# An expert's weights fetched in four pieces of 32 partitions, one piece per finished tile

## The reference

```
xn = layernorm(x)
x  = x + attention(xn) + ffn(xn)            # attention: 16 heads of 32, one shared K and V, causal
scores = sigmoid(xn @ gate_w.T)             # 32 experts in 4 groups; 2 groups, then 8 experts per token
x_lat  = xn @ fc1_w.T                       # 512 -> 256
h      = relu(x_lat @ w1[e].T) ** 2         # 256 -> 256, for each chosen expert e
y_lat += weight[token, e] * (h @ w2[e].T)   # 256 -> 256, summed over the 8 experts of a token
ffn    = y_lat @ fc2_w.T + relu(xn @ up.T) ** 2 @ down.T
```

## Time and profile before

| | |
|---|---|
| median of three runs | 1802.2 us |
| the profiled execution's own time | 1801.09 us |
| its span | 1799.3 us |
| TensorE (PE) busy | 1642.5 us, 91% |
| VectorE (DVE) busy | 1196.9 us, 67% |
| ScalarE (ACT) busy | 1068.8 us, 59% |
| GpSimd (POOL) busy | 825.5 us, 46% |
| moved by the 16 DMA engines | 277.86 MB, mean 154 GB/s |
| mean granted TensorE clock | 0.974 |

### The profile page before, as it was taken

One profiled execution on the slowest core, in us unless ns is written; L12 is line 12 of the kernel. 1 busy time (PEld: TensorE's weight loads), 2 busy tenths in 40 slices (PEclk: granted clock), 3 DMA queues, 4 the chain that ended last, 5 costly groups with the idle time before them and its releaser, 6 DMA issues.

```text
span 1799.3 us, 40017 instructions
## 1 busy us (share of the span) xinstructions
PE 1642.5 (91%) x10806; PEld 1389.0 (77%) x10806; DVE 1196.9 (67%) x3661; ACT 1068.8 (59%) x2791; POOL 825.5 (46%) x670
## 2 busy tenths in 40 slices
PE   5833999999999999999999998999999999999989
PEld 5822777777777777787777776888888988889977
DVE  6868877767868778677677784454445544455557
ACT  2322775766757757677577574666556665566642
POOL 0042532433424424334244241577677766777850
PEclk9966999999999999999999999999999999999999
DMA  7983533434334334334343334688888887888894
GB/s 279 369 308 79 153 99 117 143 103 130 124 98 144 116 110 137 106 123 132 97 149 119 122 99 138 145 162 178 171 182 171 168 181 167 175 169 153 138 258 164
DMA packets 189150, 277.86 MB, mean 154 GB/s; under 512 B 34232, under 2 KB 130623, under 8 KB 186372
## 3 DMA queue, kind: packets, MB, share of 16 engines
q0 software_dynamic: 60352, 92.59, 23.9%
q1 hardware_dynamic: 73636, 117.19, 22.0%
q10 hardware_dynamic: 54944, 65.52, 12.4%
HBM read 123.93 MB, written 131.76 MB: 142 GB/s over the span
## 4 chain that ended last, share of the span: by engine, by line
PE 57%; DMA 14%; DVE 12%; issue 7%; ACT 2%; POOL 1%; DVEq 1%; POOLq 0%; ACTq 0%; SPq 0%
DMA sums<-e_y,e_where 13%; PE m_psT L1190 7%; PE e_psH L1566 6%; PE e_psY L1577 6%; PE m_psU L64 5%; PE m_psU L66 4%; PE m_psU L65 4%; PE m_psS L1173 4%; PE m_psO L1210 4%; PE m_psY L64 4%; PE m_psY L66 4%; PE m_psY L65 4%; DVE m_sc L999 3%; PE e_psX L1551 2%; POOL sums L1531 1%
## 5 line engine op out<-in xcount | busy, mean ns | idle before, releaser
L1531 POOL DMA_INDIRECT sums<-e_y,e_where x287 | 445.7, 1553 | 202.7 <-DVE e_y L1490 123.7
L777 POOL DMA_INDIRECT slot_rows<-m_row,slots x256 | 268.4, 1048 | 553.0 <-ACT m_sc L854 509.0
L854 ACT ACTIVATE m_sc<-m_sc,m_low 128x512 f32<-128x512 f32 (+3 forms) x512 | 283.8, 557 | 154.8 <-DVE m_low L999 153.5
L1577 PE MATMUL e_psY<-e_w,e_ht 128*128 x1148 | 302.8, 387 | 25.9 <-ACT e_ht L1438 25.9
L1566 PE MATMUL e_psH<-e_xt,e_w_of 128*128 128x128 f32 x2296 | 310.3, 279 | 3.3 <-ACT e_xt L1427 3.3
L999 DVE CUSTOM_DVE_ANT_0 m_sc<-m_psS,cst 128x512 f32<-128x512 f32 (+3 forms) x512 | 229.6, 485 | 90.8 <-PE m_psS L1173 89.6
L1566 PEld LDWEIGHTS e_psH<-e_xt,e_w_of 128*128 128x128 f32 x2296 | 283.4, 194 | 5.6 <-ACT e_xt L1427 4.0
L1433 ACT ACTIVATE e_w_of<-e_w 128x512 f32 x287 | 180.8, 630 | 130.9 <-issue 122.4
L1577 PEld LDWEIGHTS e_psY<-e_w,e_ht 128*128 128x128 f32 x1148 | 198.8, 193 | 45.8 <-issue 29.6
L1487 DVE TENSOR_SCALAR e_where<-e_row,e_shifts 128x1 uint32<-128x1 uint32 x287 | 61.4, 214 | 214.0 <-DMA sums<-e_y,e_where 180.4
L1190 PE MATMUL m_psT<-cst,m_sc 128*128 128x128 f32 x1280 | 199.8, 277 | 2.0 <-ACT m_pt L865 2.0
(11 more groups left out here) (201 smaller groups left out, 3162.8 us busy)
## 6 DMA issues: line engine op xcount, KB each, us to landing
e_row<-slot_rows ACTq DMA_DIRECT2D x287, 144.5 KB, 3.5
m_qs<-m_qhi SPq DMA_DIRECT2D x256, 64.0 KB, 2.0
e_w<-in_w SPq DMA_DIRECT2D x64, 256.0 KB, 4.6
f_xt<-in_x SPq DMA_DIRECT2D x8, 1024.0 KB, 9.3
xnt_hi<-f_hi SPq DMA_DIRECT2D x8, 1024.0 KB, 4.4
xnt_lo<-f_lo SPq DMA_DIRECT2D x8, 1024.0 KB, 7.7
m_qs<-m_qlo SPq DMA_DIRECT2D x128, 64.0 KB, 2.0
sums<-empty POOLq DMA_DIRECT2D x32, 256.0 KB
```

The costliest lines, as they stand in the source:

```text
L777: pool.indirect_dma_start(out=xs, out_offset=bass.IndirectOffsetOnAxis(ap=slots_sb[:, g, k:k + 1], axis=0), in_=row[g % 2][:, :], in_offse ...
L854: nc.scalar.activation(cols, cols, ACT.Exp, bias=low[:, h % 2, i:i + 1], scale=-1.0, accum_out=total[:, h % 2, i:i + 1]).then_inc(exp_done, 1)
L1531: pool.indirect_dma_start(out=both_sums, out_offset=bass.IndirectOffsetOnAxis(ap=where[u % NY][:, 0:1], axis=0), in_=y[u % NY][:, :], in_o ...
L1577: mm = pe.matmul(psY[u % 2][:, 0:LAT], ht[u % 2][:, c * P:(c + 1) * P], w_f[:, bass.ds(e * (2 * W) + (W + c * LAT), LAT)], start=(c == 0), ...
```

## The change

An expert's two weight DMAs of 128 partitions become eight of 32 partitions. The four pairs are issued one after another; for experts 5 to 31 the pair q (q = 0, 1, 2, 3) waits until q further tiles have finished after the last tile of expert k-5. The first five experts' pieces are issued without waits between them. The two loads of `partial` follow the fourth pair, and so move back by three tiles. The semaphore count that `arrived` waits for is four times as high. Nothing else is changed.

```diff
+WP = 4
...
+            def load_part(k, q):
+                cols, rows_of = slice(k * W, (k + 1) * W), slice(q * P // WP, (q + 1) * P // WP)
+                for n, w in enumerate((w1, w2)):
+                    sp.dma_start(w_sb[rows_of, k, n, :], w[rows_of, cols]).then_inc(w_in[k % 2], 16)
+
             def load(k):
-                cols = slice(k * W, (k + 1) * W)
-                for n, w in enumerate((w1, w2)):
-                    sp.dma_start(w_sb[:, k, n, :], w[:, cols]).then_inc(w_in[k % 2], 16)
+                for q in range(WP):
+                    load_part(k, q)
 
             def arrived(k):
-                sp.wait_ge(w_in[k % 2], 32 * (k // 2 + 1))
+                sp.wait_ge(w_in[k % 2], 32 * WP * (k // 2 + 1))
                 sp.sem_inc(w_ready, 1)
...
             for k in range(AHEAD, E):
                 arrived(k - 1)
-                sp.wait_ge(y_done, end_of(k - AHEAD) + BASE)
-                load(k)
+                end = end_of(k - AHEAD)
+                for q in range(WP):
+                    sp.wait_ge(y_done, end + (BASE + q))
+                    load_part(k, q)
```

## The result

The changed kernel takes **1781.71 us** (median of five runs, 1779.58 to 1787.75) against 1802.2. The ratio to the kernel before is 0.989 with a 95% interval of 0.9857 to 0.9923: 20 us faster, and clear of no change. Measured once more on another chip it was 1780.73 us, ratio 0.988 (0.9851 to 0.991). Its profiled execution has a span of 1779.8 us.

What follows compares the result with a forecast made beforehand. Overrun, then idle DMA engines delayed scatters, costing the experts' stage 40 us against TensorE's pace. Work of 393 + 23 + 16 = 432 us at share 0.965 gives 448 instead of 468: 1801 - 20 = 1781 us, range 1760 to 1808.

Steps and rivals of the forecast that it cites:

- Work: Experts' stage: DMA engine time after the change, 393 us plus 23 for narrow width and 16 for starts, 432 us.
- the price of a piece: Weight loads: a narrow 128 KB piece (two DMAs) costs 0.56 us instead of 0.34, plus 0.10 us a DMA for starts.
- The row for the width: Attention's 64 KB query moves, nearest in shape to a narrow DMA: 236 GB/s at full share against 384 for 128 partitions.
- Share: Experts' stage: the DMA engines can hold 0.965, the middle of 0.92 without a stall and 1.01 in a burst.
- the burst of 768 KB: Weights and partial issued together: a scatter lands in 7.74 us instead of 3.41, holding VectorE, GpSimd and then TensorE.
- SyncE: Issuing queue: each issue takes about 0.42 us, six more an expert 2.5 us, hidden by 322.9 us of waits for tiles.
- The 512 KB without a stall: Last weight load, at 1618.74: the chain stays on TensorE, which speaks for bursts below 512 KB costing nothing.
- VectorE's wait for scatters: Sign in the experts' stage: the wait of VectorE's address step should fall well below 153.0 us.
- Landing of a piece: Sign at the weight loads: 2 to 3 us expected; over 5 us would speak for the pieces clogging the engines.
- No difference: Rival: starts cost 0.19 us a DMA, gain 5 us, 1796 us; or partial loads cause the stalls; chance 0.31.
- All hidden: Rival in the experts' stage: the whole 40 us loss is gained, 1761 us; chance 0.18.
- Slower: Rival at each expert's first four tiles: pieces and starts clog the DMA engines, 27 us more, 1828 us; chance 0.16.

Runs made afterwards that it cites:

- f1: Against the kernel before: eight weight DMAs of 128 partitions (64 KB each) an expert, all issued without waits for tiles; 1776.93 us, ratio 0.9852.
- e1: Against the kernel before: eight weight DMAs of 32 partitions an expert, all issued without waits for tiles; 1783.77 us, ratio 0.989.
- e2: Against the kernel before: w1 whole at the end of expert k-5, w2 whole two tiles later, then partial; 1791.25 us, ratio 0.993.
- f2: Against the kernel before: two whole weight DMAs at once, only the loads of partial moved back, by four tiles (the second by five); 1793.84 us, ratio 0.994.
- h2: Against the kernel before: four weight DMAs of 64 partitions (128 KB) an expert, without waits for tiles; 1795.46 us, ratio 0.9957.
- m1: Against the kernel before: sixteen weight DMAs of 16 partitions (32 KB) an expert, without waits for tiles; 1787.04 us, ratio 0.991.
- e4: Against the changed kernel: partial one tile after the fourth piece, the second load another tile later; 1777.86 us, ratio 0.9854 to the kernel before.
- i1: Against the changed kernel: each load of partial in four DMAs of 32 partitions at its old place; 1776.66 us, ratio 0.9851 to the kernel before.
- g1: Against the changed kernel: four 128 KB weight DMAs of 128 partitions, one per tile, and partial one tile later; 1775.77 us, ratio 0.9855 to the kernel before.

## Why the prediction was right, and where only its number was

**The time.** 1781 was forecast, 1781.71 measured, inside the forecast's own range of 1768 to 1790. Two terms of the sum were wrong, and cancelled.

- *Work.* 432 us of DMA time were expected for 217 tiles. It was 0.91 x 452 = 411 for 218: the change added some 18 us to the 393 (the rounding of the shares leaves about 5 either way), not 39. The term that was mis-sized is the price of a piece, 0.56 for its width and 0.20 for two starts. The row for the width was of moves within SBUF in a stretch that has little else; beside scatters and row loads it does not hold: eight wide DMAs and eight narrow ones used the same 1.85 us of DMA time a tile (f1, e1), and their times differ by no more than the noise. Their 0.03 us a tile over the kernel before is 6 us or so for 162 more DMAs, 0.04 each, where I took 0.10; the changed kernel's 18 is 0.11 each, and why it is more there than in e1 is open. The Trainium skill ("SBUF — State Buffer", section "Door 1: The DMA port swizzle") gives measured rates for 32 and 128 partitions, 189 and 328 GB/s; beside this kernel's other traffic that difference does not show.
- *Share.* I divided by 0.965, between a stretch without stall and a burst. Over the stage the engines held 0.91. With the true work and my share the stage would have been 426 us, less than TensorE needs; with my work and the true share 475, slower than before. That the two errors cancelled is luck.

**The mechanism.** That the burst of 768 KB stretches a scatter's landing past what three in flight can bear, and that VectorE and then TensorE stall for it, is confirmed: the landings over 6.5 us fell from 17 to one on the chain, and six other ways of slowing down the hand-over, of the weights or of `partial`, cut them to between 3 and 11 and shortened the stage (e1, e2, f1, f2, h2, m1). What I had not seen is that the change has two parts that do this. I put the gain on the waits for tiles, and priced the eight DMAs as nothing but a cost. Without the waits the gain is 0.989 all the same. The step that failed is *SyncE*: "each issue takes about 0.42 us", which I booked as hidden, is itself the brake.

**The 512 KB without a stall.** I rested "bursts below 512 KB cost nothing" on one burst of 27. f2's weights are such bursts, 512 KB with nothing right behind them, and its stage loses 32 us: the ground was wrong. For smaller bursts nothing is clear of the noise (384 KB in the changed kernel, taken apart in e4 and i1, 3 to 4 us).

**What was to be seen.** 2.06 us a tile: 2.071. DMA share 0.93 to 0.97: 0.91, too low, while the stage was shorter. VectorE's wait for scatters well below 153.0: it was 171.3, a wrong sign of a right step. GpSimd's holes over 3 us fewer: its longest wait for VectorE is 2.6 us against 4.2. Landing of a piece 2 to 3 us: the median is 2.7 in this execution but 4.3 in the kernel's other one (shortest 2.0, longest 8.1 and 8.4; a whole DMA 4.6), so the sign is not shown. ScalarE's copy of w1 must not wait for weights: it waited 8 times, 4.4 us in all, none over 1.0 (2 times and 1.1 us before), and in the kernel's other execution 3 times, 1.3 us: little, but not nothing. Nothing lost before the stage: the table came at 1108.46, but the attention ended later too in this execution (1108.0), and the first `e_y` followed 24 us after it (25 before). In the other execution these were 1106.23, 1105.8 and 25 us. With 40 DMAs the cover held, with the 80 of m1 it did not.

**Rivals.** No difference: not so, by the interval; but its second reason, that the stalls come from `partial`, was right by half, as f2's 11 us show. All hidden (1761): no run came to it; the largest stage gain, g1, still loses 10 us. Slower: the pieces cost 18 / 108 = 0.17 us more each than the bytes, far from the 0.54 more that this rival needed. The Trainium skill's rule that transfers under 64 KB pay mostly overhead ("DMA: Bandwidth & Descriptors", section "Rules for kernel authors") did not decide here: m1's DMAs of 32 KB have the smallest loss of the runs without waits (20 us), and pay before the stage.

## What to carry to other kernels

Where a prefetch has far more time than it needs and shares the DMA engines with a transfer that the path waits for, try handing it over slowly. In this kernel more and smaller DMAs on the same queue did it by the time that they take to issue, with no wait and no counting of tiles. Count that issue time as a rate (bytes per microsecond given to the engines) before booking it as hidden overhead, and look at what stands behind it on the queue. Judge a stall by the longest waits and by TensorE's pace, not by the total of a wait that has slack.

## What the runs showed of the hardware

- The DMA engines' share over a stage with three queues at work never passed 0.93 in a profile (0.84 before), though 8 us of burst stood at 1.01.
- A run of eight 64 KB DMAs on SyncE's queue mostly went out at one in 0.45 to 0.55 us; sixteen of 32 KB took 8.34 us, 0.52 us each. The price does not follow the bytes, but it is not one price for all shapes: four of 128 KB and 64 partitions took 2.43 us, 0.61 each, and two of 256 KB and 128 partitions 0.82, 0.41 each.
- Two profiled executions of the changed kernel took 1781.61 and 1777.36 us and lost 21 and 16 us in the stage, while the two medians are 1 us apart. A kernel's executions differ by that much, so one profile does not rank variants that differ by less.
